# The row of reciprocals turned by TensorE instead of sent through DRAM, w1's maximum turned likewise, GpSimd's work reordered, and the MLP's first words in five banks

## The reference

```
x = x + tanh(g_xattn) * xattn(layernorm(x), ctx, ctx)       # 16 heads of 32, softmax over 77 keys
x = x + tanh(g_ffn)   * ffn(layernorm(x))

def xattn(query, key, value):      # q, k, v = proj(.) = . @ W.T + b, by heads
    attn = softmax(q k^T / sqrt(32)) ; return (attn v) @ Wo.T + bo

def quant(x): scale = max(max|x|, 1e-6) / 127 ; return round(x / scale), scale    # one scale for the tensor
def qlinear(x, w, b): return (xq @ wq.T + b) * (sw * sx)
def ffn(x): return qlinear(gelu(qlinear(x, w1, b1)), w2, b2)                      # hidden width 2048
```

## Time and profile before

| | |
|---|---|
| time, median of 3 | 666.09 us |
| the profiled execution: time, span | 664.78 us, 662.6 us |
| granted TensorE clock, mean over the span | 0.954 |
| TensorE busy | 593.2 us (90%) |
| VectorE busy | 452.0 us (68%) |
| ScalarE busy | 334.9 us (51%) |
| GpSimd busy | 288.6 us (44%) |
| stretch of attention, hidden, output | 0 to about 412, to about 546, to 662.6 us |

### The profile page before, as it was taken

The page is one execution under the profiler, slowest core; times in us unless marked ns, Lnnn a source line. Parts: engine busy times, 40 slices in busy tenths (PEclk is TensorE's granted clock), DMA queues, the critical chain, the costliest instruction groups (busy, mean ns, idle before and its releaser), DMA issues. The chain is left out here.

```text
span 662.6 us, 9249 instructions
## 1 busy us (share of the span) xinstructions
PE 593.2 (90%) x3289; PEld 336.4 (51%) x3311; DVE 452.0 (68%) x634; ACT 334.9 (51%) x400; POOL 288.6 (44%) x240
## 2 busy tenths in 40 slices
PE   6977869595998999969799997899999999999997
PEld 6832534452654746536457566544444454444443
DVE  5934861592784887827738688498999869893271
ACT  2445244463346364452462723577777669665440
POOL 3349366098076481872842522000000535843272
PEclk8997959796998999979989998999999999999999
DMA  8457020215321221121200103887777779797764
GB/s 316 155 194 236 1 80 1 47 64 175 125 97 35 47 97 35 32 80 47 96 1 0 66 0 137 302 307 279 285 267 276 321 317 320 282 403 307 240 232 181
DMA packets 45926, 107.42 MB, mean 162 GB/s; under 512 B 6976, under 2 KB 7744, under 8 KB 41280
## 3 DMA queue, kind: packets, MB, share of 16 engines
q1 hardware_dynamic: 44544, 105.55, 44.3%
q10 hardware_dynamic: 1344, 1.37, 0.6%
HBM read 64.95 MB, written 41.96 MB: 161 GB/s over the span
## 5 line engine op out<-in xcount | busy, mean ns | idle before, releaser
L1384 PE MATMUL ps<-h_sb,w_q 128*128 (+1 forms) x476 | 108.7, 379 | 2.4 <-ACT xo L1447 1.8
L1650 PE MATMUL ps<-w_q,h_q 128*128 128x512 bf16 x441 | 96.5, 379 | 0.4
L1108 POOL TENSOR_TENSOR xr<-xr,row 128x512 f32<-128x512 f32 x28 | 37.3, 1344 | 108.9 <-DMA xr<-in_x_t 89.2
L1732 POOL TENSOR_TENSOR xo<-xo,b2s 128x512 f32<-128x512 f32 x32 | 57.3, 1821 | 61.3 <-DMA xo<-x_dram 42.8
L1384 PEld LDWEIGHTS ps<-h_sb,w_q 128*128 128x128 bf16 x488 | 46.7, 98 | 53.9 <-ACT xo L1447 2.4
L684 ACT ACTIVATE prob<-ps 77x1024 f32<-77x1024 f32 x64 | 61.7, 1014 | 23.4 <-PE ps L466 18.9
L1650 PEld LDWEIGHTS ps<-w_q,h_q 128*128 128x128 bf16 x448 | 43.8, 98 | 52.9
L1447 ACT ACTIVATE xo<-ps,b1s,sc 128x1024 f32<-128x1024 f32 x48 | 57.6, 1204 | 20.0 <-PE ps L1384 19.0
L505 PE MATMUL ps<-wo_hi,c_lo 128*128 128x512 f32 x112 | 46.1, 412 | 23.6 <-POOL c_lo L1142 23.6
L1518 DVE TENSOR_REDUCE hmax<-xo 128x1024 f32 (+1 forms) x48 | 57.0, 1212 | 9.6 <-ACT xo L1447 9.4
L424 PE MATMUL ps<-xt_hi,wq_hi 128*128 128x512 f32 x128 | 53.2, 415 | 8.4 <-DVE x L913 7.7
(11 more groups left out here) (163 smaller groups left out, 1158.2 us busy)
## 6 DMA issues: line engine op xcount, KB each, us to landing
h_dram<-xo SPq DMA_DIRECT2D x48, 512.0 KB, 2.8
h_sb<-h_dram SPq DMA_DIRECT2D x16, 1024.0 KB, 11.1
x_dram<-x SPq DMA_DIRECT2D x8, 1024.0 KB, 4.1
xo<-x_dram SPq DMA_DIRECT2D x8, 1024.0 KB, 5.1
x<-h_dram SPq DMA_DIRECT2D x8, 1024.0 KB, 8.0
x<-in_x SPq DMA_DIRECT2D x7, 1024.0 KB, 5.6
xr<-in_x_t SPq DMA_DIRECT2D x28, 256.0 KB, 4.0
out<-xo SPq DMA_DIRECT2D x7, 1024.0 KB, 5.9
```

Source lines behind the costliest of these rows:

```text
L1108: nc.gpsimd.tensor_tensor(xa, xa, row[:], ALU.mult).then_inc(xr_mul, 1)
L1384: mm = nc.tensor.matmul(ps[:, 2 * (m % 2) + s, :], w1_q[:, k, m * P:(m + 1) * P], xq_t[:, one(2 * j + s), k, :], start=(k == 0), stop=(k = ...
L1650: mm = nc.tensor.matmul(ps[:, 4 * s + t, :], h_q[s][:, m, t * P:(t + 1) * P], w2_q[:, m, :], start=(m == 0), stop=(m == MF - 1))
L1732: nc.gpsimd.tensor_tensor(xo[:, s, t, :], xo[:, s, t, :], b2s[:], ALU.add).then_inc(xb_on, 1)
```

## The change

The row no longer goes through DRAM. `row_turn` on TensorE transposes each of the four columns of `rstd1`, broadcast to 128 x 128, so that a PSUM bank (BS for chunk 1, BC for others) holds the row on all partitions; `row_copy` on ScalarE copies it to `row`. `pass_rstd` and its place in SP's queue are gone. w1's maximum over the partitions is found by a transpose of the broadcast column and a reduction on VectorE instead of GpSimd's all-reduce. In the first step the means of the weights come after the first q product, GpSimd makes `rstd` after one of four subtractions, and the low parts of the weights before the scaling of x_t. In the later steps two `c_low` stand ahead of the scaling of pieces 2 and 3. In `hidden`, the first words go through five banks, and VectorE copies three of the eight; the last product is made by halves, each with its own Gelu and maximum. A Gelu on four bytes a partition stands in `attention`'s last steps. In `output`, a product of scales comes after the roundings.

The diff, cut to its core:

```
 SP:  -  def pass_rstd(c): ...       - pass_rstd(1)   - pass_rstd(2)   - if n + 1 < NC: pass_rstd(n + 1)
 PE:
+                def row_turn(n):
+                    pe.wait_ge(ln1_rstd, rstd_value(n))
+                    if n >= 2:
+                        pe.wait_ge(c_on, GROUPS * (n - 1))
+                    for t in range(TT):
+                        mm = nc.tensor.transpose(ps[:, row_bank(n), t * P:(t + 1) * P],
+                                                 rstd1[:, t:t + 1].to_broadcast([P, P]), sh.ident[:])
+                    mm.then_inc(row_mm, 1)
 transpose_max(c):
+                    elif c < LAST:
+                        pe.wait_ge(row_on, c + 1)
 first_step():
                     project_q(0, 0)
+                    weight_means()
                     project_q(0, 1)
                     pe.wait_ge(k_split, 1)
                     scores_by_token(0, 0)
-                    weight_means()
                     project_q(0, 2)
                     scores_by_token(0, 1)
+                    row_turn(1)
                     project_q(0, 3)
...
                     scores_by_token(0, 3)
+                    pe.wait_ge(row_on, 1)
                     project_v(1, range(KD // 2))
 step(i):
                     scores_by_token(i, 0)
+                    if i < LAST:
+                        row_turn(i + 1)
                     project_q(i, 2)
...
                     sums(i, 1)
+                    if i == 1:
+                        pe.wait_ge(w1max_on, KD + 1)
+                        nc.tensor.transpose(ps[:, W1, 0:P], wmax[:, 0:1].to_broadcast([P, P]),
+                                            sh.ident[:]).then_inc(w1max_mm, 1)
                     project_out(i - 1, 0, 3, ALL)
                     scores_by_key(i, 3)
+                    if i == 1:
+                        pe.wait_ge(w1max_on, KD + 2)
 ACT:
+                def row_copy(n):
+                    act.wait_ge(row_mm, n)
+                    if n >= 2:
+                        act.wait_ge(xr_mul, KD * (n - 1))
+                    nc.scalar.copy(row[:], ps[:, row_bank(n), :]).then_inc(row_on, 1)
 first_step():  -  if m == 1: (wait wmean_mm, wq_mean)    +  if m == 2: row_copy(1)   +  if m == 0: (wait wmean_mm, wq_mean)
 step(i), after q_high(i, m):
+                        if m == 1 and nxt:
+                            row_copy(n)
 last_steps():
                     c_copy(LAST, GROUPS - 1)
+                    nc.scalar.activation(bk_sb[:, 0:1], sh.bq[:, 0:1], ACT.Gelu)
 DVE:
+                def w1_column():
                     dve.wait_ge(w1max_on, KD)
                     nc.vector.tensor_reduce(wmax[:, 0:1], w1m[:], AX.X, ALU.max).then_inc(w1max_on, 1)
-                    dve.wait_ge(w1max_all, 1)
+                def w1_scale():
+                    dve.wait_ge(w1max_mm, 1)
+                    nc.vector.tensor_reduce(wmax[:, 1:2], ps[:, W1, 0:P], AX.X, ALU.max).then_inc(w1max_on, 1)
+                    dve.wait_ge(w1max_on, KD + 2)
 step(1):  w1_column() stands behind w1_max(3), w1_scale() ahead of residual(0, 0), no longer behind it
 POOL first_step():
-                    rstd_1(1)
                     for k in range(KD): (wq_raw - wq_mean)
+                        if k == 0:
+                            rstd_1(1)
-                    scale_xt(1, 0)
-                    scale_xt(1, 1)
                     for k in range(KD): (wq_lo)
+                    scale_xt(1, 0)
+                    scale_xt(1, 1)
 POOL step(i):
                         xt_low(n, 0)
                         xt_low(n, 1)
+                        c_low(i - 1, 0)
+                        c_low(i - 1, 1)
                         scale_xt(n, 2)
                         scale_xt(n, 3)
-                    for g in range(GROUPS):
+                    for g in range(2 if nxt else 0, GROUPS):
                         c_low(i - 1, g)
-                    if i == 1: (wait w1max_on) partition_all_reduce(wmax[:, 1:2], wmax[:, 0:1], P, RMAX)
 hidden:
+        WORD_BANKS = (T0, T1, 1, 3, TW)
+        BY_DVE = (1, 3, 6)
 PE magic_words(u):
-                    if u >= 2:
-                        pe.wait_ge(xqt_on, u - 1)
+                    if u >= len(WORD_BANKS):
+                        pe.wait_ge(*words_copied(u - len(WORD_BANKS)))
 PE order:  words 0-4, half 0, 5, half 1, 6, half 2, 7   ->   words 0-3, half 0, 4, 5, half 1, 6, 7, half 2
 DVE:
+                    nc.vector.tensor_scalar(xq_t[...], words(u), -MAGIC, 1.0, ALU.add, ALU.mult).then_inc(words_dve, 1)
                 for u in range(PT): (y)
+                    if u == TT - 1:
+                        copy_words(1)
+                        copy_words(3)
...                  (b1s)
+                copy_words(6)
 last product (m = 15 of the last pass):  k inside s, h_mm, Gelu and maximum once for each half of 512
 output, DVE:  hs[4] = hs[2] * sw2 * gate moved from ahead of the 16 roundings to behind them
```

More of the change, by code:

```diff
@@ L288, in c_parts, with row_bank @@
             return (xt_hi, xt_lo) if c == LAST else (c_hi, c_lo)
+        def row_bank(n):
+            return BS if n == 1 else BC
         def rstd_value(c):
@@ L1290, in hidden @@
         xqt_on = sem("xqt_on")
+        words_act = sem("words_act")
+        words_dve = sem("words_dve")
         h_mm = sem("h_mm")
@@ L1302, in one, with words_copied, words @@
             return j if isinstance(j, int) else bass.ds(j, 1)
+        WORD_BANKS = (T0, T1, 1, 3, TW)
+        BY_DVE = (1, 3, 6)
+        def words_copied(u):
+            by_dve = sum(v <= u for v in BY_DVE)
+            return (words_dve, by_dve) if u in BY_DVE else (words_act, u + 1 - by_dve)
+        def words(u):
+            return ps[:, WORD_BANKS[u % len(WORD_BANKS)], :].rearrange("p (k n) -> p k n", k=KD)
         def first_bank(m):
@@ L1381, in step @@
                             pe.wait_ge(h_on, MF * j + m - 1)
-                        for k in range(KD):
-                            for s in range(2):
-                                mm = nc.tensor.matmul(ps[:, 2 * (m % 2) + s, :], w1_q[:, k, m * P:(m + 1) * P],
-                                                      xq_t[:, one(2 * j + s), k, :], start=(k == 0),
-                                                      stop=(k == KD - 1))
+                        by_half = last and m == MF - 1
+                        for k, s in ([(k, s) for s in range(2) for k in range(KD)] if by_half else
+                                     [(k, s) for k in range(KD) for s in range(2)]):
+                            mm = nc.tensor.matmul(ps[:, 2 * (m % 2) + s, :], w1_q[:, k, m * P:(m + 1) * P],
+                                                  xq_t[:, one(2 * j + s), k, :], start=(k == 0),
+                                                  stop=(k == KD - 1))
+                            if by_half and k == KD - 1 and s == 0:
+                                mm.then_inc(h_mm, 1)
                         mm.then_inc(h_mm, 1)
@@ L1399, in _ @@
                 idle_turns(nc, sh, TW, 12)
-                for u in range(TT + 1):
+                for u in range(TT):
                     magic_words(u)
                 half(0, 0)
+                magic_words(4)
                 magic_words(5)
@@ L1446, in step @@
                                 act.wait_ge(hmax_on, MF * j + m + 1 - RING)
+                        if last and m == MF - 1:
+                            nc.scalar.activation(dst[:, 0:CH], ps[:, bank, :], ACT.Gelu,
+                                                 bias=b1s[:, m:m + 1], scale=sc[:, 4:5]).then_inc(h_on, 1)
+                            act.wait_ge(h_mm, MF * j + m + 2)
+                            nc.scalar.activation(dst[:, CH:2 * CH], ps[:, bank + 1, :], ACT.Gelu,
+                                                 bias=b1s[:, m:m + 1], scale=sc[:, 4:5]).then_inc(h_on, 1)
+                            continue
                         nc.scalar.activation(dst.rearrange("p (s n) -> p s n", s=2),
@@ L1453, in _ @@
                 for u in range(PT):
-                    transposed(0, u)
+                    if u not in BY_DVE:
+                        transposed(0, u)
                 act.wait_ge(xs_on, 5)
@@ L1474, in _, with copy_words @@
                 dve.wait_ge(xs_on, 2)
+                def copy_words(u):
+                    dve.wait_ge(xqt_mm, u + 1)
+                    nc.vector.tensor_scalar(xq_t[:, u // TT, :, (u % TT) * P:(u % TT + 1) * P], words(u), -MAGIC, 1.0,
+                                            ALU.add, ALU.mult).then_inc(words_dve, 1)
                 for u in range(PT):
```

75 lines of the change are left out of this document (32 added, 43 removed).

## The result

The kernel after takes 610.35 us (median of 4 runs, 607.17 to 612.72), the kernel before beside it 665.92 us: a ratio of 0.916 (95% interval 0.911 to 0.921). The forecast was 615. The profiled execution of after took 611.17 us.

A forecast was written before the change was run, and what follows sets the result against it. TensorE, busy 90% of the span, was held by waits ending in GpSimd or what waits for it. Terms 8.5 + 7.0 + 15.9 + 16.9 + 2.4 = 50.7 off 664.78, plus 1.3 to the median: 615 us, range 606 to 630.

The forecast's parts named there:

- Step 0: First attention step: stop for the third exponential and its lower clock go, less the turn: 8.5 us gained.
- Step 1: Second attention step: wait for the row of maxima and its lower clock go, less clock given back and turn: 7.0 us.
- The 1.5 us that I gave back for the clock: Second attention step: two shorter waits for VectorE's maxima stay as its longest stop, costing 1.5 us of clock.
- w1's maximum: GpSimd's all-reduce: replacing it ends the residual wait and frees GpSimd of the full 19.0 us around it.
- rival C: Around the all-reduce: the 19 us belong to GpSimd whatever it runs, so the time is 628.5 us; chance 0.04.
- The forecast of 622 by that page: All-reduce idles as two code loads of about 6 us: GpSimd wins 12 us, not 19, `c_lo` 7 us later; 622 us.
- Step 2: Third attention step: excess falls from 21.4 to 5.5 us, with a `c_lo` wait of 2.0 left: 15.9 us gained.
- Steps 3 to 6: Later attention steps: earlier scaling and two early `c_lo` remove all stops, less four turns of 0.66: 16.9 us gained.
- The MLP: After attention: early Gelu table load 1.0, split last product 1.15, later product of scales 0.2, words 0: 2.4 us gained.
- A: GpSimd stays late, stops of 1 to 3 us return in steps 1, 3, 5 and 6: 627 us; chance 0.23.
- B: Attention steps: no stop at all is left and the words gain 0.7: 7 us less, so 608 us; chance 0.15.
- D: At the turns: TensorE waits for `rstd` each time, making it slower than before, 679 us at 9 us late; chance 0.02.

The follow-up runs named there:

- the run on w1 alone: Kernel before with w1's maximum by TensorE transpose and VectorE reduction, weight means after the first q product, row still through DRAM: 653.43 us, ratio 0.993.
- Before again: The kernel before, unchanged, measured and profiled again in a later comparison: 658.87 us, ratio 1.0002.
- the first order back: Kernel after with GpSimd's old first-step order: rstd ahead of the subtractions, x_t scaling ahead of wq's low parts; row still turned: 611.78 us.

## Why the prediction came out right, point by point

**Step 0, 8.5 (8.4 measured): size right, one reason wrong.** I held that the new order makes the low parts early. The turned row does it with the old order too (34.82 us), and undoing the order costs step 0 nothing (34.79).

**Step 1, 7.0 (7.2).** The row of maxima is no longer waited for, the two waits for VectorE's maxima stay at 1.6 and 1.5 us, and the turn doesn't wait. The 1.5 us that I gave back for the clock are a matter of the run: three traces show the same waits and 41.37 us at a clock of 0.96, 39.98 at 1.00 and 42.35 at 0.92. In six more traces with the turned row and the new orders it is 39.9 to 40.4, a gain of 8 us and more by the same count. That the term came out so close is in part luck.

**w1's maximum: the effect right, the account too simple.** I gave the full 19.0 us to the all-reduce and took rival C as its only opposite. Counted from the start of step 2, GpSimd scales 11.6 us earlier than before (9.7 us in, where it was 21.3), not 19.0; the rest it waits for the row's copy, and that costs nothing, because my term for step 2 was worked from ScalarE's last rounding and not from the 19.0. Both parts of the change work on the same 19.4 us. Either removed alone leaves 14 or 15 of it (14.28 without the all-reduce; 5.63 + 0.38 + 8.75 without the DRAM), both removed leave 7.8. As I had only the sum of all parts to forecast, this didn't show; for the all-reduce alone I expected 12.6 us and it was 5.0.

With the row's write gone the idle ahead of the all-reduce is 5.55 and 5.63 us, so I was wrong to take the 9.20 as its own size. The Trainium skill (GPSIMD Engine Reference, 2.1 Instruction dispatch) puts the loading of code at the first call of a freshly loaded kernel at about 6 us; the two idles agree with that, though no row shows that they are such a load. The forecast of 622 by that page fails all the same: GpSimd did win some 12 us and not 19, but its `c_lo` were not 7 us later for it.

**Step 2, 15.9 (16.6).** One stop of 2.71 us (2.0 forecast). From the end of ScalarE's last rounding, 112.77, to the first `c_lo` at 125.35 there are 12.6 us (12.0 forecast as the upper end), and TensorE stands at 122.64, 9.9 us behind the rounding (10.1 forecast). The biases took less than the 6.39 I counted (5.97); the narrowing, 2.4 us beyond the rounding and not 1.9, and `xt_lo` (2.95 us for two) took more. The 1.1 us for the later `c_lo` never came: this trace has no second stop. The rest is the turn and 1.7 us of clock (0.96), as forecast.

**Steps 3 to 6, 16.9 (18.7): the mechanism right, the turn mis-sized.** The times at which GpSimd scales and ends its first `c_lo` in step 5 came to within some 0.5 us. The turn was put at 0.66, the length of the row, and costs 0.45 between two products: 0.8 us in four steps. The other 1.0 is in the baseline: a step without a stop and without a turn takes 38.4 us (38.88 - 0.45), not the 38.7 that I made of step 4 (39.17 - 0.5). The same three products and the scores behind them, in step 4 before and after:

```profile
240.53 0.50 PE L505 MATMUL ps<-wo_hi,c_hi 128*128 128x512 f32 x1
241.72 0.50 PE L505 MATMUL ps<-wo_hi,c_lo 128*128 128x512 f32 x1 [0.46 <-POOL c_lo L1142]
242.14 0.47 PE L460 MATMUL ps<-q_hi,k_hi 32*77 32x512 f32 x4
```
```profile
204.31 0.50 PE L506 MATMUL ps<-wo_hi,c_hi 128*128 128x512 f32 x1
205.20 0.46 PE L461 MATMUL ps<-q_hi,k_hi 32*77 32x512 f32 x4
```

From the first product to the scores it is 1.61 us with the wait and 0.89 without: a wait that the profile gives as 0.46 us costs 0.72, because products that follow each other overlap (here the second starts 0.33 us behind the first, which is 0.50 long) and one behind a wait does not. So a step without a stop takes 39.17 - 0.72 = 38.45 us.

**The MLP, 2.4 (2.7 in the profiled pair, 1.8 over all traces).** From the start of the words to the first Gelu it is 11.17 us before and 8.96 after: the table load of 1.28, of which I had counted 1.0, and 0.9 of the words, which I had put at 0. The split of the last product gave 0.5 and not 1.15: I had not looked at what stands ahead of the last maximum in VectorE's own queue.

**The rivals.** A (GpSimd stays late, 627): no stop came back in steps 3, 5 or 6. B (no stop at all, 608): close, and with the four biases moved, which takes away the last stop for `c_lo`, it is 605. C (the 19 us belong to GpSimd whatever it runs): no, the wait for the residual is gone, but of the idle without the all-reduce a part stays, as the run on w1 alone shows. D (the turn waits for `rstd`): only step 1 was near, by 0.1 us. That the forecast was 4.6 us high comes from steps 3 to 6 (1.8), step 2 (0.7) and the small terms (0.4), and from the way from the trace to the median (2.1): I added 1.3 us, and this time the profiled execution lay 0.8 us above the median. Rounding 615.4 to 615 took 0.4 off.

What stays open is what GpSimd does in the idle times around the all-reduce. The second is not only the row's way back. In before SP issues the row and the pieces of x_t behind the write:

```profile
121.13 0.33 SPq L334 DMA_DIRECT2D row<-rstd_dram  x1
121.50 0.91 SPq L325 DMA_DIRECT2D xr<-in_x_t  x2
```

They take 5.7 and 6.3 us to landing, so all that the scaling waits for is there at 127.8, and it begins at 131.92, 4.1 us later. Before again gives 4.1 us as well; in the run on w1 alone, without the all-reduce, the scaling begins within 0.1 us of the landing. So some 4 us of this idle come only with the all-reduce. With the row turned the row's copy covers all of it, so that there its size can't be read; it is at most 7.56 us.

## What to carry to other kernels

When two waits end in the same idle stretch, ask what each alone would leave: the row and the all-reduce shared 19 us, and taking either one away left 14 or 15 of it. A small value that every partition needs costs some 13.6 us by way of DRAM (8.2 + 5.4), and 0.45 us of TensorE and 0.58 of ScalarE as a turn and a copy; what gained here was not only the engine that waited for it but what stood queued behind. Before splitting the last piece of a chain, look for the engine in that chain that is busy right up to it.

## What was not expected of the hardware

- A write of 2 KB, four values from each of 128 partitions, to DRAM lands after 8.2 us (median of 7); reading it back as 256 KB takes 5.4.
- The unexplained idle ahead of GpSimd's all-reduce is 5.55 and 5.63 us without that write beside it and 8.68 and 9.20 with it. That the write slows it is what these four traces suggest; no run moved the write alone.
- The clock after two stops of 1.6 and 1.5 us is not the same in every execution. In the trace of the biases moved, the sixteen idle turns behind them take 1.97 us, in after 3.06 and with the first order back 3.28:

```profile
74.95 1.97 PE L60 MATMUL ps<-ident 128*128 128x128 f32 x16
```
```profile
77.02 3.06 PE L60 MATMUL ps<-ident 128*128 128x128 f32 x16
```
```profile
77.89 3.28 PE L60 MATMUL ps<-ident 128*128 128x128 f32 x16
```

The step takes 39.97, 41.37 and 42.35 us at a mean clock of 1.00, 0.96 and 0.92. The clock ahead of step 0 differs in the same way: that stretch takes 17.32 us at 1.00 with the biases moved and 18.91 at 0.91 in after, though no edit touches it. Together these are up to 4.0 us between executions, of the size of the spread between runs of after (607.17 to 612.72). What decides it no run shows; a stop so short can cost as much in clock as in length.
